# Three attentions written out step by step, with the norm and router of the layer behind each inside its loop

## The chip, the core and the metric

The kernel runs on one core of a Trainium2 chip as one program. The metric is the device time of one execution in microseconds (us). A core has five engines, each with an instruction stream of its own that runs in order: PE (TensorE: matmuls and transposes), DVE (VectorE), ACT (ScalarE), POOL (GpSimd) and SP (SyncE, which here only issues DMAs). They are tied together by semaphores: an instruction that waits holds everything behind it on its engine.

## The reference

Four layers, each `x = x + attention(norm(x))` and then `x = x + ffn(norm(x))`, over 4096 tokens of 128 channels in 64 sequences of 64. The norm has no gain: `(x - mean) / sqrt(var + 1e-5)`. Attentions 1 to 3 are alike but for a mask in the first:

```python
q = split_heads(norm(x) @ Wq + bq)          # 16 heads of 8 channels
attn = softmax(q @ k.T * scale)             # 64 x 64 per head and sequence
x = x + join_heads(attn @ v) @ Wo + bo
```

The ffns behind them (8 experts with 2 per token; 64 grouped experts; 64 experts with a capacity) all begin with a router: `logits = norm(x) @ Wr`, with 8 or 64 columns.

## The kernel before, in words

X stays in SBUF as 32 tiles of 128 tokens. The program is a row of stages: attention 0, its output, ffn 0 (which also writes the keys and values of the three later attentions to DRAM), and then three times: a norm, a plain attention (`attention_rows`; parts at1, at2, at3 of the names in the rows), a norm with router (`layer_norm(..., router=...)`; ln3, ln5, ln7), and an ffn (ex, gr, cap). All engines meet at the end of a stage.

`pipelined` sets the order inside a stage. Each engine has a list of (lead, stage), and in step n runs each stage of the list for tile n + lead. In `attention_rows` of before, the first and last steps are written out and the middle is a loop over four tiles with addresses from a register. The lists of one step n:

- PE: `weigh`(n-1), `turn(0)`(n), `project_out`(n-2), `score`(n+1), `turn(1)`(n), `turn_o`(n-1), `project_q`(n+2).
- ACT: `take_q`(n+1), `take_o`(n-2), `exponent(0)`(n), `exponent(1)`(n).
- DVE: `top`, `shift(0)`, `shift(1)` of n, `weigh_down`(n-1), `measure`(n-3: the norm's sums), `residual`(n-2).
- POOL: `part_heads`(n+1), which multiplies the keys by head masks into KM, and `add_bias`(n+1).
- SP: `load_ahead`(n): keys K(n) after KM(n-4) is made, then values V(n) after `weigh`(n-4). K and V have four slots, and tiles 0 to 3 are loaded with the weights, ahead of the stage.

So `score`(n+1) needs KM(n+1), and that needs K(n+1) landed; K(n+1) is issued some three steps ahead of its use.

The norm with router works on groups of four tiles: DVE makes mean and root for all tiles at once (ACT gives the square root), normalises a group, PE turns it, ACT copies it to xT, PE multiplies by the router's weights, DVE copies the logits. In ln7 SP also writes the normalised rows to DRAM (`cap_rows`), one DMA for four tiles. The weights that the ffn needs (`also=loads`) are issued on SP in this norm's stage.

Of the kernel before, what the change touches and what calls it, by code (L numbers as in the profile page):

```python
# [9 lines left out]

# [536 lines left out]
def attention_rows(nc, m, part, norm, wq, wo, bq, bv, bo, keys, values, keep_mask=None):  # L547
# [8 lines left out]
    with ExitStack() as own:  # L556
# [16 lines left out]
        On, OT = sb("On", [P, HEADS, DH]), sb("OT", [P, P])  # L573
        if keep_mask is not None:
# [7 lines left out]
        def load_keys(sp, i, s):  # L582
            sp.dma_start(K[:, s, :], keys[:, bass.ds(P * i, P)]).then_inc(k_in[s], 16)

        def load_values(sp, i, s):
            v = VZ[:, s, :, :, :].rearrange("p r j w -> p (r j w)")
            sp.dma_start(v, values[bass.ds(i, 1), :, :].rearrange("a p w -> p (a w)")).then_inc(v_in[s], 16)

        def loads(sp):
# [4 lines left out]
            sp.dma_start(bias[:, :], bo.partition_broadcast(P)).then_inc(loaded, 16)  # L594
            if keep_mask is not None:
# [14 lines left out]
        TURNED, Y = slice(0, P), slice(P, 2 * P)  # L610
        chained, prepared, dots_ready = m.sem("chained"), m.sem("prepared"), m.sem("dots_ready")
# [4 lines left out]
        LOADS = 16 * (5 + (2 if keep_mask is not None else 0))  # L616
        run = lambda eng, stages: pipelined(eng, NT, stages, period=SLOTS)

        with nc.Block() as block:
            @block.sync  # L620
            def _(sp):
                def load_ahead(i, s, n):
                    if isinstance(i, int) and i < SLOTS:
# [6 lines left out]
                run(sp, [(0, load_ahead)])  # L630

            @block.gpsimd
            def _(pool):
                pool.wait_ge(prepared, 2)

                def add_bias(i, s, n):
                    mine = m.X[:, bass.ds(i, 1), :].rearrange("p a d -> p (a d)")
# [8 lines left out]
                run(pool, [(1, part_heads), (1, add_bias)])  # L646

            @block.tensor
            def _(pe):
# [3 lines left out]
                def project_q(i, s, n):  # L653
                    wait_past(pe, q_taken, i)
                    pe.matmul(psP[:, 0:P], Wq[:, :], m.xT[:, bass.ds(P * i, P)], start=True, stop=True).then_inc(q_done, 1)
# [47 lines left out]
                run(pe, [(-1, weigh), (0, turn(0)), (-2, project_out), (1, score), (0, turn(1)), (-1, turn_o), (2, project_q)])  # L703

            @block.scalar
            def _(act):
# [20 lines left out]
                run(act, [(1, take_q), (-2, take_o), (0, exponent(0)), (0, exponent(1))])  # L727

            @block.vector
            def _(dve):  # L730
# [1859 lines left out]
```

## Time and profile before

| | us |
|---|---|
| runs (median; lowest, highest) | 2042.02; 2039.81, 2051.98 |
| the profiled execution | 2055.21, of which its span 2053.4 |
| mean granted TensorE clock in it | 0.832 |

The stages around the change in the profiled execution, all times from the span's start:

| | at1 | at2 | at3 |
|---|---|---|---|
| last `top` of the attention starts | 677.73 | 1104.00 | 1708.30 |
| first work of the ffn behind the norm | 713.61 | 1137.43 | 1742.76 |

Between these two times lie the last tile's way through the attention, the meeting of the engines and the norm with router. Times are in us unless marked ns; a granted clock of 1.00 is TensorE at 2.4 GHz, 0.50 at 1.2 GHz, and a value between them is a stretch that held both.

### The profile page before, as it was taken

The numbers are of one execution on the slowest core, as the hardware profiler recorded it, in microseconds if no ns is written. First come the engines' busy times: TensorE is split into PE (matmuls) and PEld (weight loads), VectorE is DVE, ScalarE is ACT, GpSimd is POOL, SyncE is SP. The second block draws the span as 40 slices with busy tenths as digits, with TensorE's granted clock in tenths as the row PEclk, the third lists the DMA queues.
The fourth block names the chain that finished last, engine by engine and source line by source line (L and its number), as shares of the span: only waits on it lengthen the run. The fifth ranks groups of instructions, "written<-read, shape, count | busy, mean of one in ns | idle before, by whom it ended". The sixth has DMA issues, their size and how long they took to land. (4 is left out here: it accounts for less than half of the span.)

```text
span 2053.4 us, 45919 instructions
## 1 busy us (share of the span) xinstructions
PE 1617.8 (79%) x14578; PEld 1144.2 (56%) x14579; DVE 1418.5 (69%) x3509; ACT 825.6 (40%) x1722; POOL 820.6 (40%) x809
## 2 busy tenths in 40 slices
PE   5999953823688888996888699989997987179992
PEld 4777752312566655664666344437996766055551
DVE  6888866957688553437787799986776886943332
ACT  3554532778333222323343577752112343122221
POOL 3888823367233071016331000005774331047883
PEclk8999966955799699998898899999998997555555
DMA  5333302930111151112112477637993111334446
GB/s 139 82 78 78 90 2 63 283 91 0 45 47 46 43 168 39 41 35 57 45 55 58 138 306 307 266 164 263 418 415 123 56 54 52 87 80 81 82 83 149
DMA packets 242442, 241.51 MB, mean 118 GB/s; under 512 B 105698, under 2 KB 225315, under 8 KB 234915
## 3 DMA queue, kind: packets, MB, share of 16 engines
q1 hardware_dynamic: 221074, 221.02, 32.9%
q0 software_dynamic: 14336, 14.69, 3.9%
q10 hardware_dynamic: 6928, 4.49, 0.8%
q8 instruction: 56, 0.92, 0.2%
q14 instruction: 48, 0.39, 0.1%
HBM read 137.28 MB, written 100.24 MB: 116 GB/s over the span
## 5 line engine op out<-in xcount | busy, mean ns | idle before, releaser
L643 POOL TENSOR_TENSOR at_KM<-at_K,at_mask 128x512 f32<-128x512 f32 x96 | 99.8, 1039 | 301.1 <-PE at_psS L668 239.6
L718 ACT ACTIVATE at_ET<-at_psT 128x512 f32<-128x512 f32 x192 | 114.6, 597 | 245.6 <-PE at_psT L677 245.6
L753 DVE TENSOR_REDUCE at_mx<-at_psS 128x16 f32<-128x1024 f32 x96 | 117.6, 1225 | 55.0 <-PE at_psS L668 54.7
L400 POOL TENSOR_TENSOR at_E<-at_Z,at_mx 128x512 f32<-128x512 f32 x128 | 130.7, 1042 | 45.4 <-PE at_psT L445 28.4
L2058 POOL TENSOR_TENSOR gr_work<-gr_ring 128x512 f32<-128x512 f32 x96 | 121.5, 1288 | 51.7 <-DVE gr_work L2092 44.5
L690 PE MATMUL at_psO<-at_VZ,at_ET 128*64 128x18 f32 x3072 | 110.1, 215 | 40.6 <-ACT at_ET L718 40.6
L677 PE MATMUL at_psT<-kept_ident,at_Z 128*128 128x128 f32 x768 | 131.0, 295 | 10.7 <-DVE at_Z L766 5.3
L2142 PEld LDWEIGHTS gr_psY<-gr_wd,gr_work 128*128 128x128 f32 x1024 | 133.8, 192 | 5.9
L2142 PE MATMUL gr_psY<-gr_wd,gr_work 128*128 128x128 f32 x1024 | 135.8, 276 | 0.0
L690 PEld LDWEIGHTS at_psO<-at_VZ,at_ET 128*64 128x64 f32 x3072 | 101.3, 141 | 58.8 <-ACT at_ET L718 37.4
L1936 PE MATMUL gr_psV<-kept_xT,gr_wu 128*128 (+1 forms) x240 | 125.2, 604 | 0.8 <-ACT gr_V L1806 0.8
L1936 PE MATMUL gr_psV<-kept_xT,gr_wg 128*128 (+1 forms) x240 | 124.6, 601 | 0.0
L677 PEld LDWEIGHTS at_psT<-kept_ident,at_Z 128*128 128x128 f32 x768 | 84.0, 145 | 55.0 <-issue 40.2
L518 DVE TENSOR_TENSOR at_Z<-at_psS,at_amask 128x512 f32<-128x512 f32 x128 | 82.5, 686 | 42.6 <-PE at_psS L437 41.5
L2384 POOL DMA_INDIRECT cap_acc<-cap_Y,cap_idx x64 | 101.9, 1592 | 20.7 <-issue 18.9
L2423 DVE TENSOR_TENSOR cap_h<-cap_psU,cap_sg 64x128 f32<-64x128 f32 x64 | 18.1, 282 | 119.7 <-ACT cap_sg L2437 119.7
L2378 POOL DMA_INDIRECT cap_GX<-cap_rows,cap_idx x64 | 63.3, 989 | 90.9 <-DVE cap_idx L2417 77.7
L2059 POOL MEMSET gr_one<- 64x1 f32 x1 | 0.1, 91 | 247.5 <-POOLq L1781 247.5
L1817 ACT ACTIVATE gr_ring<-gr_psV,gr_bu 128x512 f32<-128x512 f32 x120 | 82.4, 687 | 31.3 <-PE gr_psV L1936 31.3
L1817 ACT ACTIVATE gr_ring<-gr_psV,gr_bg 128x512 f32<-128x512 f32 x120 | 82.4, 687 | 23.6 <-PE gr_psV L1936 23.2
L2092 DVE TENSOR_TENSOR gr_work<-gr_psF,gr_work 128x512 f32<-128x512 f32 x96 | 66.0, 688 | 33.1 <-PE gr_psY L2142 22.9
L768 DVE TENSOR_TENSOR at_Z<-at_psS,at_mx 128x512 f32<-128x512 f32 x128 | 82.5, 686 | 6.6
(556 smaller groups left out, 4205.3 us busy)
## 6 DMA issues: line engine op xcount, KB each, us to landing
gr_spill<-gr_ring SPq DMA_DIRECT2D x28, 2048.0 KB, 6.2
gr_ring<-gr_spill SPq DMA_DIRECT2D x28, 2048.0 KB, 10.2
at_amask<-mask_Bx16xSxS_ff SPq DMA_DIRECT2D x128, 128.0 KB, 2.9
kv_values<-bit_VS SPq DMA_DIRECT2D x32, 432.0 KB, 6.5
at_VZ<-kv_values SPq DMA_DIRECT2D x96, 144.0 KB, 2.1
kv_keys<-bit_KS SPq DMA_DIRECT2D x8, 768.0 KB, 6.9
at_K<-kv_keys SPq DMA_DIRECT2D x96, 64.0 KB, 1.9
cap_acc<-cap_zero SPq DMA_DIRECT2D x2, 2112.0 KB, 12.6
```

The costliest lines, as they stand in the source:

```text
L400: pool.tensor_tensor(E[:, a, :].rearrange("p (v k) -> p v k", k=SEQ), Z[:, s % 2, a, :].rearrange("p (v k) -> p v k", k=SEQ), mx[:, s % 2, ...
L518: dve.tensor_tensor(Z[:, s % 2, a, :].rearrange("p (g h e k) -> p g h e k", g=2, h=2, e=2), psS[:, 2 * a:2 * a + 2, 0:256].rearrange("p g ...
L643: pool.tensor_tensor(KM[:, s % 2, :, :], K[:, s, :].unsqueeze(1).broadcast_to([P, 4, P]), mask4[:, :].unsqueeze(2).broadcast_to([P, 4, P]) ...
L677: last = pe.transpose(psT[:, r * P:r * P + P], Z[:, a, r * P:r * P + P], m.ident[:, :])
L690: last = pe.matmul(psO[rows, t * PW:t * PW + PW], ET[:, 4 * a + r, rows], VZ[:, s, PAIRS * b + t, :, :].rearrange("p j w -> p (j w)"), sta ...
L718: act.activation(ET[:, 4 * a:4 * a + 4, :].rearrange("p r q -> p (r q)"), psT[:, :], ACT.Exp, scale=QK_SCALE).then_inc(exped, 1)
L753: dve.tensor_reduce(mx[:, :].rearrange("p (g v) -> p g v", v=4), psS[:, :, 0:256].rearrange("p g (v k) -> p g v k", k=SEQ), AX.X, ALU.max) ...
L1817: act.activation(ring[:, u, j % TILES, :], psV[:, j % 4, :], ACT.Silu if is_up else ACT.Identity, bias=bias).then_inc(taken, 1)
L1936: pe.matmul(psV[:, j % 4, :], w, m.xT[:, bass.ds(512 * g, 512)], start=True, stop=True).then_inc(multiplied, 1)
L2058: pool.tensor_tensor(tp[:, s % 4, :], ring[:, s // 4, first, :], ring[:, s // 4, first + 1, :], ALU.mult).then_inc(pooled, 1)
L2142: last = pe.matmul(psY[:, j, :], h[:, s % 2, j * P:j * P + P], wd[:, s, :], start=False, stop=(s == C - 1), skip_group_check=True)
L2384: pool.indirect_dma_start(accs[s % ACCS], bass.IndirectOffsetOnAxis(ap=idx2[:, s:s + 1], axis=0), Y[:, s % 4, :], None, compute_op=ALU.add ...
```

## The change

`attention_rows` is written out for all tiles, without a loop. The three norms with router are gone as stages; their work stands in the attention's lists, tile by tile: `aggregate` on DVE (-3), a reciprocal root by Newton steps on POOL for each group of four tiles (`invert`, -4; the last group by DVE behind its list), `normalise` on ACT (-9), `turn_hat` on PE (-10), `take_hat` on ACT (-10), `route` on PE (-10), `take_logits` on ACT (-11). On SP the ffn's loads stand ahead of `load_ahead`, and in at3 `write_row`(-9) stands behind it. The calls and some buffers move accordingly.

```diff
+def invert_std(eng, chain, m, g, moments, shift, work):
+    mine = slice(4 * g, 4 * g + 4)
+    v, y, t = (work[:, n, :] for n in range(3))
+    chain.link(eng.tensor_scalar(v, moments[:, mine, 1], EPS, None, ALU.add))
+    eng.tensor_scalar(y.bitcast(I32), v.bitcast(I32), -0.5, GUESS, ALU.mult, ALU.add)
+    chain.link(eng.tensor_scalar(v, v, -0.5, None, ALU.mult))
+    for _ in range(3):
+        chain.link(eng.tensor_tensor(t, y, y, ALU.mult))
+        chain.link(eng.tensor_tensor(t, t, v, ALU.mult))
+        chain.link(eng.tensor_scalar(t, t, 1.5, None, ALU.add))
+        chain.link(eng.tensor_tensor(y, y, t, ALU.mult))
+    eng.tensor_scalar(m.rstd[:, mine], y, 1.0, None, ALU.mult)
+    eng.tensor_scalar(m.mean[:, mine], moments[:, mine, 0], 1.0, None, ALU.mult)
+    chain.link(eng.tensor_tensor(t, moments[:, mine, 0], y, ALU.mult))
+    return eng.tensor_scalar(shift[:, mine], t, -1.0, None, ALU.mult)
...
+        xh, newton = sb("xh", [P, SLOTS, D]), sb("newton", [P, 2, 3, 4])
...
-        run = lambda eng, stages: pipelined(eng, NT, stages, period=SLOTS)
+        run = lambda eng, stages: pipelined(eng, NT, stages, period=SLOTS, unrolled=True)
...
                 def load_ahead(i, s, n):
-                    if isinstance(i, int) and i < SLOTS:
+                    if i < SLOTS:
                         return
                     sp.wait_ge(km_ready, i - (SLOTS - 1))
                     load_keys(sp, i, s)
                     sp.wait_ge(summed, i - (SLOTS - 1))
                     load_values(sp, i, s)
 
-                run(sp, [(0, load_ahead)])
+                def write_row(i, s, n):
+                    if rows is not None:
+                        sp.wait_ge(hat_ready, i + 1)
+                        sp.dma_start(rows[i], xh[:, s, :]).then_inc(rows_out[s], 16)
+
+                if also:
+                    also(sp)
+                run(sp, [(0, load_ahead), (-9, write_row)])
...
-                run(pool, [(1, part_heads), (1, add_bias)])
+                def invert(i, s, n):
+                    if s == SLOTS - 1 and n < LAST:
+                        pool.wait_ge(moments_ready, i + 1)
+                        invert_std(pool, newtons, m, n, moments, shift_by, newton[:, 0]).then_inc(inverted_std, 1)
+
+                run(pool, [(1, part_heads), (1, add_bias), (-4, invert)])
...
-                run(pe, [(-1, weigh), (0, turn(0)), (-2, project_out), (1, score), (0, turn(1)), (-1, turn_o), (2, project_q)])
+                def turn_hat(i, s, n):
+                    pe.wait_ge(hat_ready, i + 1)
+                    wait_past(pe, logits_taken, i)
+                    pe.transpose(psP[:, HAT], xh[:, s, :], m.ident[:, :]).then_inc(hat_turned, 1)
+
+                def route(i, s, n):
+                    pe.wait_ge(hat_taken, i + 1)
+                    pe.matmul(psP[:, LOGITS], m.xT[:, P * i:P * i + P], Wr[:, :], start=True, stop=True).then_inc(routed, 1)
+
+                run(pe, [(-1, weigh), (0, turn(0)), (-2, project_out), (1, score), (-10, turn_hat), (0, turn(1)), (-1, turn_o),
+                         (-10, route), (2, project_q)])
...
-                run(act, [(1, take_q), (-2, take_o), (0, exponent(0)), (0, exponent(1))])
+                def normalise(i, s, n):
+                    if n < LAST:
+                        act.wait_ge(inverted_std, n + 1)
+                    else:
+                        act.wait_ge(inverted_last, 1)
+                    wait_past(act, hat_turned, i - (SLOTS - 1))
+                    if rows is not None:
+                        wait_past(act, rows_out[s], 16 * n)
+                    act.activation(xh[:, s, :], m.X[:, i, :], ACT.Identity, bias=shift_by[:, i:i + 1], scale=m.rstd[:, i:i + 1]).then_inc(hat_ready, 1)
...
+                run(act, [(1, take_q), (-11, take_logits), (-2, take_o), (-9, normalise), (0, exponent(0)), (-10, take_hat), (0, exponent(1))])
...
-                run(dve, [(0, top), (0, shift(0)), (0, shift(1)), (-1, weigh_down), (-3, measure), (-2, residual)])
+                run(dve, [(0, top), (0, shift(0)), (0, shift(1)), (-1, weigh_down), (-3, measure), (-2, residual), (-3, aggregate)])
+                dve.wait_ge(moments_ready, NT)
+                invert_std(dve, chain, m, LAST, moments, shift_by, newton[:, 1]).then_inc(inverted_last, 1)
...
-        layer_norm(nc, m, "ln3", router=(t["L1_ffn_w_router"], prob), also=loads)
+        attend(router=(t["L1_ffn_w_router"], prob), also=loads)
...
-            layer_norm(nc, m, "ln5", router=(t["L2_ffn_Wr"], S), also=loads)
+            attend(router=(t["L2_ffn_Wr"], S), also=loads)
...
-            layer_norm(nc, m, "ln7", router=(t["gate_wT"], L), rows=tiles_of(rows)[:, :, 0:D])
+            attend(router=(t["gate_wT"], L), rows=tiles_of(rows)[:, :, 0:D])
```

Three places show how instructions move. The first is SP in at3, the end of its list before: keys (L583) and values (L587) alone, then the stage ends, and the norm's stage loads its router weights (L200) and writes the rows (L206).

```order
L583 DMA at_K<-kv_keys 128x128
L587 ISA
L587 DMA at_VZ<-kv_values 128x288
L121 REGISTER_ALU
L121 COMPARE_AND_BRANCH
L619 UNCONDITIONAL_BRANCH
L197 UNCONDITIONAL_BRANCH
L200 DMA ln7Wr<-gate_wT 128x64
L206 DMA cap_rows<-ln7xh 128x4x128 x8
```

SP in at3 after the change: keys (L610), values (L614) and row writes (L667), from K(8) to the third row.

```order
L610 DMA at_K<-kv_keys 128x128
L614 DMA at_VZ<-kv_values 128x288
L610 DMA at_K<-kv_keys 128x128
L614 DMA at_VZ<-kv_values 128x288
L667 DMA cap_rows<-at_xh 128x128
L610 DMA at_K<-kv_keys 128x128
L614 DMA at_VZ<-kv_values 128x288
L667 DMA cap_rows<-at_xh 128x128
L610 DMA at_K<-kv_keys 128x128
L614 DMA at_VZ<-kv_values 128x288
L667 DMA cap_rows<-at_xh 128x128
```

Six pairs of K and V (tiles 4 to 9) come without a row. From K(10) on one row write stands ahead of every K: row n-9, then K(n+1), V(n+1), row n-8. Twenty-two of K(10) to K(31) stand so, and the last ten rows follow together.

The second is ACT in at3, one step. Before: the take of q (L712), of the turned output (L725), and the two halves of the exponential (L718).

```order
L712 ACTIVATE at_Q<-at_psP,at_bq 128x128
L725 ACTIVATE at_OT<-at_psY 128x128
L718 ACTIVATE at_ET<-at_psT 128x512 x2
L712 ACTIVATE at_Q<-at_psP,at_bq 128x128
L725 ACTIVATE at_OT<-at_psY 128x128
L718 ACTIVATE at_ET<-at_psT 128x512 x2
```

And after, where `cap_L` is the logits, `at_xh` the normalised tile and `kept_xT` its turned copy:

```order
L772 ACTIVATE at_Q<-at_psP,at_bq 128x128
L803 ACTIVATE cap_L<-at_psP 128x64
L785 ACTIVATE at_OT<-at_psY 128x128
L795 ACTIVATE at_xh<-kept_X,at_shift,kept_rstd 128x128
L778 ACTIVATE at_ET<-at_psT 128x512
L799 ACTIVATE kept_xT<-at_psP 128x128
L778 ACTIVATE at_ET<-at_psT 128x512
```

The normalised tile is the fourth instruction behind the second exponential of the step before, and the first exponential of its own step comes behind it.

The third is PE in at3, one step after the change; without L756 (`turn_hat`) and L760 (`route`) it is the step of before.

```order
L740 MATMUL at_psO<-at_VZ,at_ET 64x18 x16
L727 MATMUL at_psT<-kept_ident,at_Z 128x128 x4
L751 MATMUL at_psY<-at_Wo,at_OT 128x128
L718 MATMUL at_psS<-at_KM,at_Q 64x256 x8
L756 MATMUL at_psP<-kept_ident,at_xh 128x128
L727 MATMUL at_psT<-kept_ident,at_Z 128x128 x4
L747 MATMUL at_psY<-kept_ident,at_On 128x128
L760 MATMUL at_psP<-at_Wr,kept_xT 128x64
L705 MATMUL at_psP<-kept_xT,at_Wq 128x128
```

`turn_hat` came between the score of tile n+1 and the second turn of tile n, `route` ahead of the projection of q.

## Rows read from the trace of the kernel before

**Rows 1.** Windows: us, busy (x count) of PE, PEld, DVE, ACT, POOL, PEclk, DMA, GB/s.

```profile
420.00:510.00 90.00, 30.00 (x232) 22.37 (x232) 60.06 (x146) 74.14 (x93) 75.06 (x32) 0.50 0.08 21
677.70:713.60 35.90, 28.05 (x181) 25.62 (x180) 16.75 (x63) 8.69 (x16) 0.00 (x0) 0.55 0.09 25
1104.00:1137.40 33.40, 20.61 (x181) 18.44 (x179) 18.15 (x62) 8.70 (x16) 0.00 (x0) 0.77 0.59 105
1603.00:1708.00 105.00, 93.45 (x1655) 74.13 (x1647) 91.80 (x189) 43.70 (x108) 37.74 (x52) 1.00 0.19 53
1708.30:1742.80 34.50, 26.14 (x181) 24.08 (x179) 18.23 (x62) 8.73 (x17) 0.04 (x1) 0.61 0.21 63
```

**Rows 2.** Timeline of at3, DVE: `top` of tiles 4 and 31 (start, duration).

```profile
1603.25 1.23 DVE L753 TENSOR_REDUCE at_mx<-at_psS 128x16 f32<-128x1024 f32 x1 [0.39 <-PE at_psS L668]
...
1708.30 1.23 DVE L753 TENSOR_REDUCE at_mx<-at_psS 128x16 f32<-128x1024 f32 x1 [0.29 <-PE at_psS L668]
```

**Rows 3.** Timeline of one step of at3 at full clock.

```profile
1651.20 1.11 PE L690 MATMUL at_psO<-at_VZ,at_ET 128*64 128x18 f32 x32 [0.55 <-ACT at_ET L718]
...
1652.49 0.33 SPq L587 DMA_DIRECT2D at_VZ<-kv_values  x1
...
1653.05 0.69 PE L668 MATMUL at_psS<-at_KM,at_Q 32*64 32x256 f32 x16
...
1653.36 0.34 SPq L583 DMA_DIRECT2D at_K<-kv_keys  x1
...
1653.67 0.65 PE L677 MATMUL at_psT<-kept_ident,at_Z 128*128 128x128 f32 x4
...
1653.95 1.04 POOL L643 TENSOR_TENSOR at_KM<-at_K,at_mask 128x512 f32<-128x512 f32 x1 [2.56 <-PE at_psS L668]
...
1654.36 0.60 ACT L718 ACTIVATE at_ET<-at_psT 128x512 f32<-128x512 f32 x1 [0.83 <-PE at_psT L677]
1654.85 0.36 ACT L712 ACTIVATE at_Q<-at_psP,at_bq 128x128 f32<-128x128 f32 x1
...
1655.10 0.28 ACT L725 ACTIVATE at_OT<-at_psY 128x128 f32<-128x128 f32 x1
```

**Rows 4.** Timeline of one step of at2 at half clock.

```profile
987.34 1.16 PE L668 MATMUL at_psS<-at_KM,at_Q 32*64 32x256 f32 x16
...
988.42 1.11 PE L677 MATMUL at_psT<-kept_ident,at_Z 128*128 128x128 f32 x4
...
989.54 0.64 PE L655 MATMUL at_psP<-kept_xT,at_Wq 128*128 128x128 f32 x2
...
990.21 0.37 ACT L712 ACTIVATE at_Q<-at_psP,at_bq 128x128 f32<-128x128 f32 x1
```

**Rows 5.** ACT's normalise in ln6, durations in ns min/median/max.

```profile
L265 ACT ACTIVATE ln6xh<-kept_X,ln6shift,kept_rstd x8: 479/492/505, 1572.3 to 1578.2; 128x128 f32<-128x128 f32 x8
```

**Rows 6.** Timeline of ln7, PE: eight router passes, two for a tile.

```profile
1724.54 1.80 PE L300 MATMUL ln7psL<-ln7Wr,kept_xT 128*128 128x64 f32 x8
```

**Rows 7.** DMA issues, all K loads: count, KB, median us to landing.

```profile
at_K<-kv_keys SPq DMA_DIRECT2D x96, 64.0 KB, 1.9
```

**Rows 8.** The first four K loads of at2, each with a V load behind it.

```profile
L583 SPq DMA_DIRECT2D at_K<-kv_keys x4: 431/432/442, 966.8 to 969.7; - x4
...
DMA to landing us min/median/max: 2.8/3.2/3.5
```

**Rows 9.** Timeline of at1's end: the last tile's output turned, and added to X.

```profile
686.44 0.18 PEld L697 LDWEIGHTS at_psY<-kept_ident,at_On 128*128 128x128 f32 x1 [0.74 <-DVE at_On L776]
...
688.11 0.29 DVE L782 TENSOR_TENSOR kept_X<-kept_X,at_psY 128x128 f32<-128x128 f32 x1 [1.46 <-PE at_psY L701]
```

**Rows 10.** Timeline of ln5, SP: first and last of the grouped ffn's loads.

```profile
1114.54 0.43 SPq L1753 DMA_DIRECT2D gr_br<-L_ffn_br  x1
...
1136.25 0.53 SPq L1762 DMA_DIRECT2D gr_bd<-L_ffn_bdown  x1
```

**Rows 11.** Costliest groups: POOL's smallest operation, us and mean ns.

```profile
L1611 POOL TENSOR_TENSOR ex_spare<-ex_zero 128x1 f32<-128x1 f32 x32 | 6.5, 203 | 138.4 <-DVE ex_idx L1636 137.8
```

More of the change, by code:

```diff
@@ L9 @@
 from contextlib import ExitStack
+from functools import partial
 import concourse.bass as bass
@@ L544, in _, with attention_rows @@
                 run(dve, [(0, add_masks), (-2, invert), (0, top(0)), (-2, weigh_down), (0, top(1)), (-2, add_halves)])
-def attention_rows(nc, m, part, norm, wq, wo, bq, bv, bo, keys, values, keep_mask=None):
+GUESS = float(0x5F3759DF)
+def invert_std(eng, chain, m, g, moments, shift, work):
[13 more added lines that the diff above has]
+    return eng.tensor_scalar(shift[:, mine], t, -1.0, None, ALU.mult)
+def attention_rows(nc, m, part, norm, wq, wo, bq, bv, bo, keys, values, keep_mask=None, *, router, also=None, rows=None):
     m.part = part
@@ L573, in attention_rows @@
         On, OT = sb("On", [P, HEADS, DH]), sb("OT", [P, P])
+        wr, logits = router
+        E = logits.shape[2]
+        Wr = sb("Wr", [P, E])
+        xh, newton = sb("xh", [P, SLOTS, D]), sb("newton", [P, 2, 3, 4])
+        moments, shift_by = sb("moments", [P, NT, 2]), sb("shift", [P, NT])
         if keep_mask is not None:
@@ L615, in attention_rows @@
         y_ready, x_added = m.sem("y_ready"), m.sem("x_added")
-        LOADS = 16 * (5 + (2 if keep_mask is not None else 0))
-        run = lambda eng, stages: pipelined(eng, NT, stages, period=SLOTS)
+        measured, moments_ready, newton_chained, inverted_std, inverted_last, hat_ready = (m.sem(n) for n in (
+            "measured", "moments_ready", "newton_chained", "inverted_std", "inverted_last", "hat_ready"))
+        hat_turned, hat_taken, routed, logits_taken = (m.sem(n) for n in ("hat_turned", "hat_taken", "routed", "logits_taken"))
+        rows_out = [m.sem(f"rows_out{u}") for u in range(SLOTS)] if rows is not None else None
+        LAST = NT // 4 - 1
+        LOADS = 16 * (6 + (2 if keep_mask is not None else 0))
+        run = lambda eng, stages: pipelined(eng, NT, stages, period=SLOTS, unrolled=True)
         with nc.Block() as block:
@@ L628, in load_ahead @@
                     load_values(sp, i, s)
-                run(sp, [(0, load_ahead)])
+                def write_row(i, s, n):
[5 more added lines that the diff above has]
+                run(sp, [(0, load_ahead), (-9, write_row)])
+                for s in range(SLOTS if rows is not None else 0):
+                    sp.wait_ge(rows_out[s], 16 * NT // SLOTS)
             @block.gpsimd
@@ L1745, in grouped_ffn @@
             eq, sel, rank, excl = (sb(n, [P, NG], on=routing) for n in ("eq", "sel", "rank", "excl"))
-            ones = sb("ones", [P, HALF], on=routing)
             count, cols = sb("count", [P, 4], on=routing), sb("cols", [P, 8], on=routing)
@@ L2525, in program @@
         m.free_sems()
-        attention_rows(nc, m, "at1", "ln2", *(t["L1_xattn_" + n] for n in ("wq", "wo", "bq", "bv", "bo")), keys[0], values[:, 0],
-                  keep_mask=t["mask_1x1xSxS2_ik1"])
+        attend = partial(attention_rows, nc, m, "at1", "ln2", *(t["L1_xattn_" + n] for n in ("wq", "wo", "bq", "bv", "bo")),
+                         keys[0], values[:, 0], keep_mask=t["mask_1x1xSxS2_ik1"])
+        expert_ffn(nc, m, t, attend)
         m.free_sems()
-        expert_ffn(nc, m, t)
+        attend = partial(attention_rows, nc, m, "at2", "ln4", *(t["L2_xattn_" + n] for n in ("WqT", "WoT", "Wq_b", "Wv_b", "Wo_b")),
+                         keys[1], values[:, 1])
+        grouped_ffn(nc, m, t, attend)
         m.free_sems()
-        attention_rows(nc, m, "at2", "ln4", *(t["L2_xattn_" + n] for n in ("WqT", "WoT", "Wq_b", "Wv_b", "Wo_b")), keys[1], values[:, 1])
-        m.free_sems()
-        grouped_ffn(nc, m, t)
-        m.free_sems()
-        attention_rows(nc, m, "at3", "ln6", *(t["L3_xattn_" + n] for n in ("Wq", "Wo", "bq", "bv", "bo")), keys[2], values[:, 2])
-        m.free_sems()
-        capacity_ffn(nc, m, t)
+        attend = partial(attention_rows, nc, m, "at3", "ln6", *(t["L3_xattn_" + n] for n in ("Wq", "Wo", "bq", "bv", "bo")),
+                         keys[2], values[:, 2])
+        capacity_ffn(nc, m, t, attend)
 def lay_out(inputs):
```

33 lines of the change are left out of this document (23 added, 10 removed).

## The prediction, as recorded before the changed kernel was run

> **What bounds the kernel now.** I read three views: the windows by stage, then the timeline of single steps, then the DMA and group lists. The windows [rows 1] give two kinds of stretch. In the loop of at3 PE is busy 93.45 of 105 us at clock 1.00, DVE 91.80; the two engines hand each other one tile after the other, and a tile takes (1708.30 - 1603.25) / 27 = 3.89 us [rows 2]. Behind the last tile come 35.9, 33.4 and 34.5 us of drain, engines' meeting and router norm, in which PE works 20.6 to 28.1 us, much of it at half clock. These 103.8 us are what the change can shorten; the loops are what it can lengthen, 96 tiles in all. One step of at3 [rows 3] shows what is not on the path now: K's issue at 1653.36 is for a tile three steps ahead, and KM at 1653.95, which starts when a buffer comes free (2.56 us behind PE), is for the score after next. So the chain from K over KM to the score has more than two steps in hand.
>
> The trace has another thing that matters: SP is one stream. V's issue at 1652.49 comes 0.18 us after `weigh` ends (1651.20 + 1.11), for it waits for a `weigh`, and the next K, whose own wait was over long before, is issued only behind it at 1653.36 [rows 3]. A wait of SP holds what is queued behind it.
>
> **The drains.** Removed: three norms with router as stages. Added: the last tiles' norm in the drain of the attention. The last `top` of at1 starts at 677.73, and the last residual ends at 688.40 [rows 9], 10.7 us later. Behind it the lists go on to lead -11, nine steps more. Each is PE turn, ACT copy, PE route, ACT copy, one after the other, since `turn_hat` waits for the logits of the tile before. The nearest rows are turn, copy, projection, add: 686.44 to 688.11, 1.67 us, and 0.30 for the last operation, so 1.97 at half clock. With 0.9 for the aggregate and the end (estimate: three operations of the size of the DVE row) [rows 9] the drain is 10.7 + 9 x 1.97 + 0.9 = 29.3 us. The same is taken for all three: saved are 6.6, 4.1 and 5.2, together **15.9 us**. Bounds: nothing saved; or the PE half of each round (0.9 us) halved at full clock, some 4 us more each. DVE's own inversion of the last group lies beside the first of these rounds, which still handle earlier tiles; without that cover it would add about 4 us a drain.
>
> **The loops of at1 and at2.** PE gets one transpose (a quarter of 0.65 = 0.16 us) ahead of `turn(1)`, and the router pass in a gap in which PE waits for ACT anyway. ACT gets three operations, and is idle over half of the time [rows 1]. What goes is the loop's own register work; I put the step at 3.94 against 3.89 us, 27 x 0.05 = **+1.4** in at2, and nothing in at1, whose mask makes its step longer. DVE's aggregate lies in the wait of DVE for the score (0.29 to 0.39 us) [rows 2]. If it didn't fit, it would cost about 0.2 x 96 = 19 us, which I hold unlikely.
>
> POOL's inversion is 19 small operations for four tiles. The smallest POOL operation in the trace takes 203 ns [rows 11]: 3.9 us at least; with a hand-over of 0.1 us (taken) at each of 15 chained ones 5.4; with the 0.21 that POOL took to follow PE (1653.74 to 1653.95) [rows 3] 7.0. It starts behind the aggregate, some 0.75 us after a score's start, and KM (1.04, and 0.2 to start) must be made two scores later: 2 x 3.89 - 0.75 - 1.24 = 5.8 us. So at 5.4 it is hidden and costs nothing; the cover is thin.
>
> **The ffn's loads.** In at2 SP now issues the grouped ffn's weights ahead of K(4): 1114.54 to 1136.78 in the trace, 22.2 us [rows 10]. Until K(4) is needed there are four tiles preloaded, four steps of 3.9 to about 6 us at half clock, and the pipeline's start. K(4) comes late by 0 to 6.6 us; **+3**.
>
> **The row writes in at3.** Before, eight DMAs behind the loop; now 32. For 22 tiles, K(10) to K(31), the write of row n-9 stands on SP ahead of K(n+1). It waits for `normalise`(n-9), which ACT does in step n, as the fourth instruction behind the last exponential of step n-1. K(n+1) must then be issued, land, be made into KM and scored, all in that same step n, since PE's list has `score`(n+1) ahead of `turn(1)`(n). The three steps in hand are gone, and a closed ring is left, one turn for a tile: score, `turn_hat`, `turn(1)`, exponential, `take_q`, `take_logits`, `take_o`, `normalise`, row issue, K issue, landing, KM, score. Behind SP's wait stands K, and for K wait POOL, PE and so all.
>
> At full clock [rows 3]: score to `turn(1)` 0.62, `turn_hat` 0.16, `turn(1)` to the end of the exponential 1.29 (1653.67 to 1654.96). `take_q` starts 0.11 before that end, the three behind it at 0.25 each (1654.85 to 1655.10), and `normalise` takes 0.49 [rows 5]: 1.13. SP: 0.18 to wake, 0.48 from one issue to the next (966.8 to 969.7 holds six) [rows 8], landing 2.2. The landing has a median of 1.9 when K goes nearly alone [rows 7] and 2.8 to 3.5 in a burst of eight [rows 8]; here K has one row write ahead of it and one V behind, nearer to alone. So 2.86. KM 1.04 and two hand-overs, 0.15 together (PE to ACT took 0.04, PE to POOL 0.21): 1.19. Sum 0.62 + 0.16 + 1.29 + 1.13 + 2.86 + 1.19 = **7.25 us**, 3.36 more than 3.89.
>
> At half clock [rows 4]: 1.08 and a quarter of 1.11 to `turn(1)`. Then `project_q` ends last: 989.54 + 0.64 - 988.42 = 1.76, with a router pass ahead of it (1.80 / 4 = 0.45) [rows 6]; `take_q` 0.03 later, 0.75 and 0.49 to the end of `normalise`. With SP and POOL as above: 1.08 + 0.28 + 1.76 + 0.45 + 0.03 + 0.75 + 0.49 + 2.86 + 1.19 = **8.89 us**, 5.00 more.
>
> Which clock? In the ring PE stands still for the 4 us from `normalise` to KM in every step. The stretches of the trace with such gaps ran at 0.50, 0.55, 0.61 and 0.77, the dense loop at 1.00 [rows 1]. I take half clock: 22 x 5.00 = **+110**.
>
> The Trainium skill has a sentence that speaks against a cost here: in "Trainium Kernel Development and Optimization", Key Constraints, it says that DMAs issued from several engines run on the same 16 DMA engines, and that spreading them saves only the sequencer's issue time. By that, rows on SP cost SP's issue time alone, and the +110 would be nothing. V ahead of K [rows 3] shows that the wait in front of an issue also counts.
>
> **Sum.** -15.9 + 1.4 + 3 + 110 = +98.5, and a few tenths for the ten other steps of at3: +99. The profiled execution is 2055.2 us (span 2053.4 and 1.8 around it), which makes 2154; it lies 13 us above the median of the runs, 2042.0, for which I get **2141 us**. Its own range: landing 1.9 to 3.2 gives -7 to +22, the drains -13 to +16, K(4) 3 either way; not all at one end, 2129 to 2165.
>
> **The rivals.**
> 1. The ring turns at full clock: 22 x 3.36 = 74 in place of 110, **2105 us** (2093 to 2129). For it: PE's work in a step is dense once it starts. Against it: the windows named above. Chance 0.20.
> 2. POOL is late too. If a chained operation costs the 0.21 hand-over, the inversion takes 7.0 us against 5.8 of cover, and 1.2 us are lost for each of seven groups in at1 and at2 (at3 has time to spare): +17, **2158 us**. It decides at 5.8 us. For it: no chain of small POOL operations is in the trace. Against it: the 203 ns. Chance 0.12.
> 3. Not slower: SP's wait for the row is over before K is due, so that the rows cost 22 x 0.48 = 11 us of an SP that is idle anyway. The place is K's issue in at3. What decides is the time from `normalise` to the score, 2.86 + 1.19 = 4.05 us. Between the end of the exponential (1654.96) and the score one step after 1653.05 lie about 2.0 us, and `normalise` itself ends 1.13 after the exponential, so 0.9 us are there for 4.05. For it: the sentence above, and that K was three steps early. Then -15.9 + 4.4 + 1.4 = -10 is left: **2032 us**. Chance 0.08.
> 4. The norm inside the drain saves nothing, the ring is there: +16 on the forecast, inside its range; no chance of its own.
>
> **How the numbers follow.** Half clock 0.60, full clock 0.20, POOL late 0.12, rows harmless 0.08. The range 2093 to 2168 takes in the first two with their bounds and most of the third, and leaves out the last. A measurement of this kernel can tell about 1% (20 us) from no change: 2032 is within it, and faster only if the drains come out at their best too. Faster 0.03, within 1% 0.06, slower 0.91.
>
> **What would show it.** In at3 of the changed kernel the distance between two `top`s should be 3.9 us up to about tile 9 and then 8.9 (7.25 at clock 1.00) to tile 31, each K issue right behind a row issue, each row issue waiting for `normalise`, POOL's KM waiting for K's landing and no more for PE, and the granted clock down to 0.50. At2 should keep 3.9 to 4.0 and begin with one gap at tile 4. From last `top` to the ffn's first work there should be about 29 us. The forecast is wrong if the `top`s of at3 stay at 4 us, if KM still waits for PE there, or if POOL's inversion shows up as a wait for KM in every fourth step of at2.

## The result, and the profile after

| | us |
|---|---|
| kernel before: median (lowest, highest) | 2044.98 (2039.81, 2051.98) |
| changed kernel: median (lowest, highest) | 2128.59 (2126.46, 2133.61) |
| ratio, 95% interval | 1.041 [1.037, 1.045] |
| forecast (range) | 2141 (2093 to 2168) |
| profiled execution of the changed kernel, span, clock | 2126.46, 2124.7, 0.808 |

The change makes the kernel 4.1% slower. Where the time goes is read from a few marks in both traces: the first and the last `top` of each attention, and the first work of the ffn behind it.

| us | before | after | difference |
|---|---|---|---|
| start to the norm ahead of at1 (nothing changed there) | 520.8 | 514.5 | -6.3 |
| at1, first to last `top` | 141.85 | 139.42 | -2.4 |
| at2, first to last `top` | 125.48 | 136.81 | +11.3 |
| at3, first to last `top` | 123.21 | 217.45 | +94.2 |
| last `top` to the ffn, at1, at2, at3 | 35.9, 33.4, 34.5 | 25.1, 25.7, 29.5 | -10.8, -7.7, -4.9 |
| all else (norms ahead, the three ffns) | | | -2.1 |
| span | 2053.4 | 2124.7 | +71.3 |

The windows of the changed kernel (start:end, us, busy of PE, PEld, DVE, ACT and POOL, granted clock, DMA share, GB/s) show at2's loop, at3's ring and the three drains.

```profile
1003.00:1096.90 93.90, 91.58 (x1526) 72.98 (x1525) 84.73 (x193) 57.25 (x158) 56.13 (x158) 1.00 0.19 52
1606.00:1786.00 180.00, 137.28 (x1402) 109.22 (x1401) 79.72 (x177) 54.12 (x150) 52.25 (x142) 0.57 0.13 35
1786.00:1815.50 29.50, 21.30 (x121) 15.70 (x121) 8.59 (x37) 11.99 (x40) 3.28 (x16) 0.50 0.08 23
1096.90:1122.60 25.70, 16.33 (x121) 11.34 (x119) 8.44 (x37) 11.78 (x40) 3.71 (x19) 0.67 0.00 1
668.80:693.90 25.10, 16.09 (x121) 11.90 (x121) 8.72 (x38) 11.27 (x40) 3.65 (x19) 0.64 0.00 1
```

At2's loop is as dense as at3's was [rows 1], with the norm's work in it. At3 is another stretch: PE idle for 43 of 180 us and its clock down to 0.57, while DMA has less to do than before (35 against 53 GB/s). No engine is busy throughout and no DMA is the bound there; something waits. One turn at half clock, from the timeline, chosen rows in order of time:

```profile
1740.27 0.50 ACT L795 ACTIVATE at_xh<-kept_X,at_shift,kept_rstd 128x128 f32<-128x128 f32 x1
1740.79 0.32 SPq L667 DMA_DIRECT2D cap_rows<-at_xh  x1
1741.15 0.43 SPq L610 DMA_DIRECT2D at_K<-kv_keys  x1
...
1743.17 1.04 POOL L686 TENSOR_TENSOR at_KM<-at_K,at_mask 128x512 f32<-128x512 f32 x1 [6.60 <-DMA at_K<-kv_keys]
...
1744.27 1.16 PE L718 MATMUL at_psS<-at_KM,at_Q 32*64 32x256 f32 x16 [1.26 <-POOL at_KM L686]
...
1745.36 0.47 PE L756 MATMUL at_psP<-kept_ident,at_xh 128*128 128x128 f32 x1
...
1745.62 1.06 PE L727 MATMUL at_psT<-kept_ident,at_Z 128*128 128x128 f32 x4
...
1747.01 0.68 PE L705 MATMUL at_psP<-kept_xT,at_Wq 128*128 128x128 f32 x2
...
1747.73 0.37 ACT L772 ACTIVATE at_Q<-at_psP,at_bq 128x128 f32<-128x128 f32 x1 [0.41 <-PE at_psP L705]
...
1748.26 0.50 ACT L795 ACTIVATE at_xh<-kept_X,at_shift,kept_rstd 128x128 f32<-128x128 f32 x1
...
1748.78 0.32 SPq L667 DMA_DIRECT2D cap_rows<-at_xh  x1
```

Read the starts from top to bottom: each row follows the one above it, when that has ended or landed; PE's rows overlap a little, and short ones that are not shown lie between some of them. `normalise` ends at 1740.77, the row is issued 0.02 us later, K 0.36 after it, KM starts 2.02 us after K's issue, the score 1.10 after KM's start, and 8.0 us after the first row write comes the next. Against the step of before [rows 3], KM no longer waits for PE to free a buffer but for K's landing. The same holds for all tiles of the ring. The view of POOL's KM gives how often it ran, what ended POOL's idle time before it, and who waited for it (total us, times):

```profile
L686 POOL TENSOR_TENSOR at_KM<-at_K,at_mask x22: 1040/1040/1041, 1610.0 to 1783.6; 128x512 f32<-128x512 f32 x22
...
  DMA at_K<-kv_keys: 121.9, 22
...
  PE at_psS L718: 42.3, 22
```

All 22 KMs wait for K, 121.9 us together, and 22 scores wait for KM, 42.3 us. K itself is not slow to land:

```profile
L610 SPq DMA_DIRECT2D at_K<-kv_keys x22: 320/432/865, 1608.1 to 1781.7; - x22
...
DMA to landing us min/median/max: 1.8/2.0/3.4
```

A median of 2.0 us against 1.9 before [rows 7]: it is issued late. The distance between `top`s is 3.8 us from the fourth to the ninth step, then 6.6, and from there between 7.9 and 9.5; 8.19 on average over the 22 steps between these two:

```profile
1605.78 1.23 DVE L831 TENSOR_REDUCE at_mx<-at_psS 128x16 f32<-128x1024 f32 x1 [0.30 <-PE at_psS L718]
...
1786.00 1.23 DVE L831 TENSOR_REDUCE at_mx<-at_psS 128x16 f32<-128x1024 f32 x1 [2.04 <-PE at_psS L718]
```

In the longest steps K landed later. In the one of 9.24 us it took 3.2 us from K's issue to KM:

```profile
1632.54 0.43 SPq L610 DMA_DIRECT2D at_K<-kv_keys  x1
...
1635.73 1.04 POOL L686 TENSOR_TENSOR at_KM<-at_K,at_mask 128x512 f32<-128x512 f32 x1 [2.46 <-DMA at_K<-kv_keys]
```

At2 lost 11 us at one place, its fifth tile. SP and POOL there:

```profile
959.40 7.99 SPq L1840 DMA_DIRECT2D gr_wg<-L_ffn_Wgate  x1
967.85 6.83 SPq L1841 DMA_DIRECT2D gr_wd<-L_ffn_Wdown  x1
...
976.84 0.52 SPq L1844 DMA_DIRECT2D gr_bd<-L_ffn_bdown  x1
977.41 0.58 SPq L610 DMA_DIRECT2D at_K<-kv_keys  x1
...
981.83 1.04 POOL L686 TENSOR_TENSOR at_KM<-at_K,at_mask 128x512 f32<-128x512 f32 x1 [15.90 <-DMA at_K<-kv_keys]
...
984.19 1.22 DVE L831 TENSOR_REDUCE at_mx<-at_psS 128x16 f32<-128x1024 f32 x1 [8.23 <-PE at_psS L718]
```

K(4) is issued behind the grouped ffn's weights and lands 4.4 us later, beside their traffic (DMA is busy 0.82 of this step). The step is 11.75 us long, and three more follow at 6.2 us, at half clock:

```profile
984.20:1002.80 18.60, 18.46 (x184) 14.51 (x184) 10.95 (x25) 5.19 (x12) 5.39 (x11) 0.50 0.13 35
```

The kernel before has 125.48 in the table, and some 4 us of it are a start of at2 at half clock (steps of 5.76 and 6.19), which this execution of the changed kernel did not have; the run with the loads behind, below, is the cleaner comparison.

### The profile page after: what moved, and what is told of

Its sections match the earlier page's. It is cut to its first block and busy times, and to the rows that moved or that the text cites. A ratio compares the mean times of both kernels' runs of the same rounds, so it can differ in the third digit from the quotient of the medians.

```text
span 2124.7 us, 45141 instructions
## 1 busy us (share of the span) xinstructions
PE 1668.8 (79%) x14578; PEld 1171.9 (55%) x14579; DVE 1400.7 (66%) x3518; ACT 887.1 (42%) x1978; POOL 902.0 (42%) x1208
## 5 line engine op out<-in xcount | busy, mean ns | idle before, releaser
L727 PE MATMUL at_psT<-kept_ident,at_Z 128*128 128x128 f32 x768 | 147.0, 323 | 7.3 <-DVE at_Z L844 2.9
L740 PE MATMUL at_psO<-at_VZ,at_ET 128*64 128x18 f32 x3072 | 123.7, 226 | 12.7 <-ACT at_ET L778 10.6
L740 PEld LDWEIGHTS at_psO<-at_VZ,at_ET 128*64 128x64 f32 x3072 | 113.9, 157 | 31.9 <-ACT at_ET L778 27.6
L718 PE MATMUL at_psS<-at_KM,at_Q 32*64 32x256 f32 x1536 | 81.5, 487 | 51.0 <-POOL at_KM L686 51.0
L727 PEld LDWEIGHTS at_psT<-kept_ident,at_Z 128*128 128x128 f32 x768 | 101.8, 164 | 28.3 <-issue 16.9
L2507 DVE TENSOR_TENSOR cap_h<-cap_psU,cap_sg 64x128 f32<-64x128 f32 x64 | 18.1, 283 | 118.4 <-ACT cap_sg L2521 118.4
```

Source lines behind the costliest of these rows:

```text
L727: last = pe.transpose(psT[:, r * P:r * P + P], Z[:, a, r * P:r * P + P], m.ident[:, :])
L740: last = pe.matmul(psO[rows, t * PW:t * PW + PW], ET[:, 4 * a + r, rows], VZ[:, s, PAIRS * b + t, :, :].rearrange("p j w -> p (j w)"), sta ...
```

## The experiments

The theory: at3's loss is the wait of SP for the normalised row, with K queued behind it, and at2's is K(4) behind the weights. The rivals: the row writes cost by issue and traffic; the written-out code or the added work on ACT and PE is slow in itself; the half clock is a cause of its own. Ratios are to the kernel before, run beside each; the `top` distances are of one profiled execution each.

**Keys ahead.** SP's loads three tiles earlier; row writes, their place and their waits untouched.

```diff
-                run(sp, [(0, load_ahead), (-9, write_row)])
+                run(sp, [(3, load_ahead), (-9, write_row)])
```

> The changed kernel, with one number changed: SP's list runs the K and V loads three tiles ahead (lead 3 in place of 0). The row write of at3 keeps its place on SP, its wait for the normalised tile and its traffic. Theory (a row's wait on SP holds K back, and a ring score - normalise - row - K - KM - score is left): K(n+3) is now issued behind row n-10 and has two steps in hand, so at3's 22 steps fall from 8.19 us to 3.9: 22 x 4.3 = 94 us less, about 2034 us. Rival (the 32 row writes cost by their own issue and traffic, or ACT's and PE's added work makes the step long): nothing of that has changed, the steps stay near 8.2 and the time near 2128.

Measured: 2032.41 us, ratio 0.991 [0.989, 0.994]. At3's steps are 3.81 and 3.92, its `top`s 123.36 us apart in place of 217.45. POOL's waits in 70 us of at3 (total us, times, longest):

```profile
POOL at_newton L555 <- DVE at_moments L868: 10.6, 5, 2.1
POOL at_KM L686 <- PE at_psS L718: 9.9, 4, 2.5
```

KM waits for PE again, as before the change [rows 3], and never for K between the first and the last `top` of at3, though one K took 3.9 us to land. SP still waits for every row; nobody needs what stands behind it at once. All 94 us of at3 are gone with one number.

**Rows later.** Eight buffers for normalised tiles, the row written three steps later, between the same K loads.

```diff
-        xh, newton = sb("xh", [P, SLOTS, D]), sb("newton", [P, 2, 3, 4])
+        HATS = 2 * SLOTS
+        xh, newton = sb("xh", [P, HATS, D]), sb("newton", [P, 2, 3, 4])
...
-                run(sp, [(0, load_ahead), (-9, write_row)])
+                run(sp, [(0, load_ahead), (-12, write_row)])
```

> The changed kernel with the normalised tiles in eight buffers in place of four, and the row write of at3 at lead -12 in place of -9: the same 32 DMAs at the same place between the K loads on the same queue, but each for a tile that was normalised three steps before. Theory (it is the wait for normalise that holds SP): the wait is over when SP comes to it, K is on time, at3's steps fall to 3.9 us, about 2034 us. Rival (issue and traffic of the rows): 8.2 us a step and 2128 stay. If both the wait and the issue count, the steps come out between, by 0.4 to 0.5 us for each row issue: 2044.

Measured: 2030.95 us, 0.993 [0.990, 0.996]; steps 3.81 and 3.92. SP's timeline in the ring:

```profile
1651.14 0.32 SPq L615 DMA_DIRECT2D at_VZ<-kv_values  x1
1651.50 0.43 SPq L668 DMA_DIRECT2D cap_rows<-at_xh  x1
...
1651.97 0.43 SPq L611 DMA_DIRECT2D at_K<-kv_keys  x1
```

The row stands ahead of K as in the changed kernel and costs 0.47 us of SP, and no step is longer for it. So it is the wait, and not the row's issue or traffic.

**Rows from ACT.** The same writes on ACT's queue, behind the second exponential.

```diff
-                run(sp, [(0, load_ahead), (-9, write_row)])
+                run(sp, [(0, load_ahead)])
...
+                def write_row(i, s, n):
+                    if rows is not None:
+                        act.wait_ge(hat_ready, i + 1)
+                        act.dma_start(rows[i], xh[:, s, :]).then_inc(rows_out[s], 16)
...
-                run(act, [(1, take_q), (-11, take_logits), (-2, take_o), (-9, normalise), (0, exponent(0)), (-10, take_hat), (0, exponent(1))])
+                run(act, [(1, take_q), (-11, take_logits), (-2, take_o), (-9, normalise), (0, exponent(0)), (-10, take_hat), (0, exponent(1)), (-9, write_row)])
```

> The changed kernel with the 32 row writes of at3 issued by ACT, behind the second exponential of the step that normalised the tile, in place of SP; K and V alone on SP. Theory (K is held back by the wait that stands ahead of it in the same stream): the ring opens, at3's steps fall to 3.9 to 4.3 us (ACT spends 0.3 to 0.4 us on each issue and was idle 0.6 us or more before each exponential), 2030 to 2042 us. Rival, after the sentence of the Trainium skill that another issuing engine saves only the sequencer's issue time: 22 x 0.36 = 8 us less, about 2120 us.

Measured: 2031.06 us, 0.992 [0.989, 0.995]; at3's steps 3.92. Another queue gave 97 us, not the 8 of the issue time. The sentence of the Trainium skill ("Trainium Kernel Development and Optimization", Key Constraints) that issuing from several engines saves only the sequencer's issue time gives no more than those 8; here the measurement decides against it as a price. In "DMA: Bandwidth & Descriptors" (Anatomy of one DMA — SWDGE (gpsimd) path) the Trainium skill says that a semaphore wait happens on the issuing sequencer, before dispatch. That section is on DMAs of GpSimd; the trace shows the same for SP, where the row's issue follows the end of `normalise` by 0.02 us (1740.77, 1740.79) and K's comes 0.36 behind it.

**Clock fill.** The changed kernel with five idle matmuls a step on PE ahead of the score, in at3 from tile 10 on.

```diff
+                def fill(i, s, n):
+                    if rows is not None and i >= 10:
+                        for _ in range(5):
+                            pe.matmul(psP[:, 3 * P:4 * P], m.ident[:, :], m.ident[:, :], start=True, stop=True)
...
-                run(pe, [(-1, weigh), (0, turn(0)), (-2, project_out), (1, score), (-10, turn_hat), (0, turn(1)), (-1, turn_o),
+                run(pe, [(-1, weigh), (0, turn(0)), (-2, project_out), (0, fill), (1, score), (-10, turn_hat), (0, turn(1)), (-1, turn_o),
```

> The changed kernel, and in at3 from tile 10 on five more matmuls a step on PE ahead of the score, whose result nobody uses: they fill the gap in which PE waits for KM. The ring stays as it is. Theory (part of the ring's 8.19 us is TensorE's half clock, which the gaps bring about): the granted clock of at3's ring rises from 0.57 to near 1.00 and the step falls to about 6.7 us (the forecast's 7.25 for full clock less the 0.5 us by which the trace's SP part is shorter), 22 x 1.5 = 33 us less: about 2096 us. Rival (the clock is not what the gaps decide, or the ring's length is all in SP, ACT and POOL): the clock stays near 0.57, the added matmuls lie in the gap or lengthen the step by up to 2 us: 2128 to 2170.

Measured: 2110.61 us, 1.031 [1.027, 1.035], so 18 us less than the changed kernel (ratio 1.041), with more work. The window of the ring, and one turn in it:

```profile
1612.00:1772.00 160.00, 121.33 (x1609) 101.12 (x1609) 77.84 (x176) 54.07 (x150) 51.60 (x140) 0.90 0.14 40
1701.66:1708.28 6.62, 5.07 (x78) 4.21 (x75) 3.54 (x9) 2.50 (x7) 1.45 (x2) 1.00 0.14 42
```

The granted clock went from 0.57 to 0.90, and the step from 8.19 to 7.30 us ((1772.1 - 1611.5) / 22). The turn shown lies between two row writes, 6.62 us apart, wholly at clock 1.00. So the theory's 6.7 is there, in some of the steps. The others are longer for two reasons: three steps of about 8 us ran at clock 0.54 to 0.57, and in five steps of 7.4 to 8.1 us at clock 1.00 K took 2.9 to 3.5 us to land in place of 2.0. Of the 4.3 us that a step of the ring lost, 1.4 are the half clock (8.0 against 6.62, K landing in 2.0 us in both), some 0.2 what later landings add on average (8.19 against 8.0), and 2.7 the ring itself, which is there at either clock.

**Loads behind.** The changed kernel with the ffn's weights behind the K and V loads.

```diff
-                if also:
-                    also(sp)
                 run(sp, [(0, load_ahead), (-9, write_row)])
+                if also:
+                    also(sp)
```

> The changed kernel with the ffn's weight loads of SP behind the K and V loads in place of ahead of them; at3's rows as in the changed kernel. Theory (the grouped ffn's weights hold K(4) of at2 back by 7 us and the half clock then lasts three tiles longer): at2 goes back from 136.8 us between its first and last top to about 126, so 10 us less, 2118 us. Rival (the weights are needed at the ffn's start and only wait in another place): the grouped ffn begins late by what at2 gains, and the time stays at 2128.

Measured: 2119.67 us, 1.035 [1.030, 1.040]. At2's `top`s are 121.35 us apart in place of 136.81; the fifth step is 3.81 us long in place of 11.75, and no half clock follows. So K(4) behind the weights is the cause of at2's loss. The stretch gains 15.5 us where 10 were expected; the medians differ by 9, as do the two profiled executions, in which the unchanged part ahead of at1 took 3.3 us more here and the grouped ffn 2.5. That ffn took 433.3 to 436.1 us whether the loads stood ahead or behind (436.1 in keys ahead, too), so that it waits for its weights is not what shows; the gain stays.

**Unrolled only.** The kernel before with its attentions written out, and nothing else (the same edit as in the change: `unrolled=True` and constant addresses).

```diff
-        run = lambda eng, stages: pipelined(eng, NT, stages, period=SLOTS)
+        run = lambda eng, stages: pipelined(eng, NT, stages, period=SLOTS, unrolled=True)
```

> The kernel before, with its three attentions written out without a loop and with constant addresses, and nothing else: the norms with router stay stages of their own. Theory (the loop's registers cost little and its removal gains little: the changed kernel's at1 lost 2.4 us between first and last top): steps of 3.81 in place of 3.89 us in 24 steps of each of three attentions, 5 to 6 us less, 2039 us. Rival (written-out code is slow in itself, for there are more instructions to fetch, and that is part of the loss): more than 2045 us.

Measured: 2036.75 us, 0.997 [0.994, 1.000]: no slower, and not surely faster. The steps of at2 and at3 are 3.81 and 3.82, as expected, where the loop had 4.00 at every second pair. Written-out code is no part of the loss. Beside the 3.92 of the changed kernel it also prices the norm inside the loop: 0.11 us a step in at2, and nothing in at1 (4.51 here, 4.41 to 4.51 in the changed kernel).

**Long inverse.** Keys ahead, and six Newton steps in place of three, to measure the cover over POOL's inversion.

```diff
-    for _ in range(3):
+    for _ in range(6):
         chain.link(eng.tensor_tensor(t, y, y, ALU.mult))
```

> The kernel with K and V three tiles ahead on SP, and six Newton steps in place of three in the inversion (twelve more chained operations of 0.28 us: POOL's inversion takes 8.6 us in place of 5.2; the last group's, on DVE, about 2.4 us more). It measures the cover over POOL's inversion. By the forecast's 5.8 us of cover POOL would make KM 2.8 us late once in four steps, 7 x 2.8 us in each of at1, at2 and at3: 59 us more than 2032, about 2090 us. Rival (KM is made a tile further ahead than the forecast took, so the cover is 9 us or more): 2032 to 2036 us, with no wait for KM on PE.

Measured: 2136.85 us, 1.043 [1.038, 1.048]: 104 us slower than keys ahead, more than either expected. In at2 every fourth step is 6.4 us long and the one behind it mostly 5.7 to 6.7. PE's waits in 100 us of at2 (total us, times, longest), then the clock in a window of at2 and in two steps, one with such a wait and the one behind it:

```profile
PE at_psS L718 <- POOL at_KM L686: 9.1, 4, 2.6
```

```profile
1060.00:1130.00 70.00, 63.11 (x826) 51.01 (x825) 45.99 (x104) 32.00 (x90) 37.73 (x120) 0.77 0.15 42
...
1052.78:1059.15 6.37, 3.95 (x66) 3.10 (x66) 3.55 (x9) 2.50 (x7) 5.21 (x20) 1.00 0.19 56
1059.15:1065.39 6.24, 6.24 (x65) 4.93 (x65) 3.64 (x8) 2.50 (x7) 2.38 (x4) 0.54 0.10 27
```

From the inversion's first operation to the KM behind it POOL takes 8.6 us here, and in at2 and at3 PE then mostly waits 2.4 for that KM (1.7 to 2.6). So the cover in at2 is about 8.6 - 2.4 = 6.2 us, near the forecast's 5.8, and the rival's 9 was wrong. The waits of all three attentions are 17, together 36 us (six in at1, six in at2, five in at3; the seventh inversion of an attention has no KM behind it), while the `top`s of the three lie 96 us further apart than in keys ahead. The rest came with the clock, in the step of the wait or the one to three behind it, which ran wholly or partly at half clock: a gap of PE in a dense loop cost 2.7 times its length here.

**Both moved.** Keys ahead and loads behind.

```diff
-                if also:
-                    also(sp)
-                run(sp, [(0, load_ahead), (-9, write_row)])
+                run(sp, [(3, load_ahead), (-9, write_row)])
+                if also:
+                    also(sp)
```

> The changed kernel with the K and V loads three tiles ahead on SP and the ffn's weight loads behind them, nothing else. Theory (the two losses stand in different places and add): 2032 less the 10 us of at2: about 2022 us, 1.2% under the kernel before, with steps of 3.8 to 3.9 us in at2 and at3 and no gap at at2's fifth tile. Rival (what at2 gains is given back because the weights come late for the grouped ffn): 2032 us.

Measured: 2021.88 us, 0.988 [0.985, 0.991]. At2 121.36 us, at3 123.27: the two losses add. The change is worth 1.2% once SP's list is in order, against 0.3% for the written-out loops alone.

**Drain overlapped.** Both moved, and the last ten tiles turn and route in the banks of the scores, the router pass one step later.

```diff
+        FREE = NT - 10
+        hat_at = lambda i: psP[:, P:2 * P] if i < FREE else psS[:, i % 4, 0:P]
+        logits_at = lambda i: psP[:, 2 * P:2 * P + E] if i < FREE else psS[:, i % 4, P:P + E]
+        early = lambda stage: lambda i, s, n: stage(i, s, n) if i < FREE else None
+        late = lambda stage: lambda i, s, n: stage(i, s, n) if i >= FREE else None
...
-                         (-10, route), (2, project_q)])
+                         (-10, early(route)), (-11, late(route)), (2, project_q)])
...
-                run(act, [(1, take_q), (-11, take_logits), (-2, take_o), (-9, normalise), (0, exponent(0)), (-10, take_hat), (0, exponent(1))])
+                run(act, [(1, take_q), (-11, early(take_logits)), (-12, late(take_logits)), (-2, take_o), (-9, normalise), (0, exponent(0)), (-10, take_hat), (0, exponent(1))])
```

> As the kernel with both loads moved, and the last ten tiles of each attention turn and route in the four PSUM banks that the scores have left free, with the router pass one step behind the turn, so that PE turns tile i+1 while ACT copies tile i. Theory (the drain is a chain PE - ACT - PE - ACT of 1.8 to 1.9 us a tile, nine times in each attention): a round falls to about 1.2 us, 9 x 0.6 x 3 = 16 us less, one round more of 1.2 x 3 = 4 us: 12 us less, about 2010 us. Rival (PE alone takes 1.1 us a round at half clock and ACT 1.0, and the rounds in the first half lie beside the last tile's attention, so little is left): 2022 us.

Measured: 2000.41 us, 0.977 [0.973, 0.980], the fastest of all, and 21.5 us less than both moved, where 12 were expected. One round of the drain in the changed kernel (at3), and then in this one:

```profile
1802.90 0.69 PE L760 MATMUL at_psP<-at_Wr,kept_xT 128*128 128x64 f32 x2 [0.37 <-ACT kept_xT L799]
1803.62 0.22 ACT L803 ACTIVATE cap_L<-at_psP 128x64 f32<-128x64 f32 x1 [0.78 <-PE at_psP L760]
1803.74 0.48 ACT L795 ACTIVATE at_xh<-kept_X,at_shift,kept_rstd 128x128 f32<-128x128 f32 x1
...
1803.99 0.45 PE L756 MATMUL at_psP<-kept_ident,at_xh 128*128 128x128 f32 x1 [0.41 <-ACT cap_L L803]
...
1804.48 0.28 ACT L799 ACTIVATE kept_xT<-at_psP 128x128 f32<-128x128 f32 x1 [0.25 <-PE at_psP L756]
```

```profile
1688.11 0.60 PE L764 MATMUL at_psS<-at_Wr,kept_xT 128*128 128x64 f32 x2
1688.19 0.48 ACT L799 ACTIVATE at_xh<-kept_X,at_shift,kept_rstd 128x128 f32<-128x128 f32 x1
1688.58 0.27 ACT L803 ACTIVATE kept_xT<-at_psS 128x128 f32<-128x128 f32 x1
...
1688.73 0.47 PE L760 MATMUL at_psS<-kept_ident,at_xh 128*128 128x128 f32 x1
1688.75 0.22 ACT L807 ACTIVATE cap_L<-at_psS 128x64 f32<-128x64 f32 x1
...
1689.00 0.59 PE L764 MATMUL at_psS<-at_Wr,kept_xT 128*128 128x64 f32 x2
```

In the first, leaving out the normalise (L795), each row waits for the one above it, and a round takes 1.91 us. In the second, ACT works beside PE, and this round takes 0.89 at the same half clock; those of at3 take 0.67 to 0.88 from logits to logits. Once in each drain 1.8 to 2.3 us pass: the normalise of the last group now waits for DVE's inversion (1.2 us in at3), which the slower rounds had covered. From last `top` to ffn there are 17.8, 17.9 and 18.1 us in place of 24.8, 25.3 and 25.3 in both moved: 21.6 us, as much as the medians differ. The two profiled executions differ by 14.2 us only, for at1 and at2 of this one began with steps at half clock and are 11.7 us longer from first to last `top`.

## Why the prediction was right, and where its sizes were off

**The ring in at3: right, 15 us too large.** Forecast 22 x 5.00 = 110 at half clock, measured 22 x 4.30 = 95 (8.19 - 3.89). Its start at tile 10, its members and KM's wait came as described, and the three kernels that part K from the row's wait take it away. The size: from `normalise`'s end to KM's start the sum had 2.86; the trace has 2.40 (0.02 to wake, 0.36 to K's issue, 2.02 to land). From `take_q` to `normalise` ACT takes 0.53 (1747.73 to 1748.26), not three times 0.25, when the inputs are ready; KM and its hand-over take 1.10, not 1.19. That is 0.77 of the 0.9 us by which the quiet steps of 8.0 are below 8.89; steps of 8.4 to 9.5, in most of which K took 2.4 to 3.4 us to land, make the 8.19. Such landings are there in keys ahead too (up to 3.9 us) and cost nothing there; the ring puts each of them on the path.

**The clock: right for most of the stretch, for a reason that was too strong.** 0.57 was granted; 15 of the 22 steps ran at 0.50. But PE does not stand still for 4 us a step: `weigh`, the first `turn` and `project_out` lie in that gap, and PE was idle for 43 of 180 us, 1.9 a step. The forecast chose the clock by likeness to the windows of [rows 1], and the choice came out; the length of the standstill it had wrong. The rival at full clock (7.25 us a step, 2105 us) did not come about; filled, a full-clock step is 6.62, with the same 0.6 us too much in the sum.

**The drains: 23.4 saved, 15.9 forecast.** The round was forecast at 1.97 and took 1.77 in at1 and 1.91 in at2 and at3. At3, wholly at half clock, came out at 29.5 against 29.3, and that close only by luck: the last residual ended 12.8 us behind the last `top` in place of 10.7, and eight full rounds of 1.91 followed in place of nine of 1.97. In at1 and at2 the first rounds lie beside the last tile's own way through the attention (there are eight left when it is through, not nine), at a clock of 0.64 and 0.67, so they end 4 us earlier.

**At2's loads: the term that failed.** Forecast +3 with an upper bound of 6.6; the stretch lost 11.3, and 15.5 against the kernel with the loads behind. Two parts were missing: K(4) lands 4.4 us after its issue beside the weights' traffic, not 1.9, and behind the gap of PE that it leaves three more tiles run at half clock. The bound counted the issue time alone.

**The loops and POOL: right but for at1.** Steps of 3.92 in at2 (3.94 forecast); what the loop's registers cost, 0.08, and what the norm adds, 0.11, nearly cancel. At1 was put at nothing and gained 2.4. The inversion, from its first operation to the KM behind it, takes 5.2 us (5.4 forecast):

```profile
1033.87 0.23 POOL L555 TENSOR_SCALAR at_newton<-at_moments 128x4 f32<-128x4 f32 x1 [2.14 <-DVE at_moments L868]
...
1038.88 0.22 POOL L566 TENSOR_SCALAR at_shift<-at_newton 128x4 f32<-128x4 f32 x1
1039.07 1.04 POOL L686 TENSOR_TENSOR at_KM<-at_K,at_mask 128x512 f32<-128x512 f32 x1
```

PE waits for no KM in at2's loop, so it is hidden. By the long inverse the cover is about 6.2 us and not 5.8, so 1.0 us of it is left; and a late POOL would have cost more than the rival's sum, which counts the waits alone (six a stretch, not seven) and no half clock behind them.

**The sum.** The loss was 84 us in the medians (2128.59 - 2044.98); in the profiled pair it is 71.3 + 6.3 = 77.6 us behind the unchanged front. The forecast was 99, put on a median of 2042.02 from three runs; with a fourth the median of the kernel before is 2044.98. From that to 77.6 lead the ring (-16), the drains (-7.5), at1's loop (-2.4), the rest (-2.1) and, the other way, at2 (+6.9: 11.3 in place of 3 + 1.4). The 6.9 us that were missing in at2 hid a part of what the ring and the drains had too much, so the sum came out better than its terms, by luck.

## What to carry to other kernels

When a DMA with a wait is put into a queue, look at what stands behind it and when that is needed: a wait in front of a prefetch can turn it into a load on demand, and whatever makes the wait end then joins a ring with whatever needs the load. Moving the prefetch ahead in the list, or the waiting write back by a few steps, costs a number or a buffer. And price a gap of PE in a dense loop with the steps that follow it: at2's late K cost 1.3 to 2.2 times its gap in four of the kernels here, and the long inverse 2.7 times its gaps.

## What the runs showed of the hardware

- A late arrival costs at the clock as well: behind one 8 us gap at2 ran three steps at clock 0.50, 6.2 us each in place of 3.8; behind gaps of 7.7 to 8.6 us at the same place it was one step in rows later, two in keys ahead and four in rows from ACT.
- Two queued DMAs of SP are issued 0.36 us apart when SP has just waited (1740.79, 1741.15) and 0.47 when it hasn't; SP's issue follows the end of ACT's `normalise` by 0.02 to 0.03 us, and the end of PE's `weigh` by 0.18 [rows 3].
- Large loads hold SP itself, and what is queued behind them: the issues of the grouped ffn's gate and down weights took 7.99 and 6.83 us of its time each, against 0.43 for small ones.
- Small POOL operations of 128 x 4 elements take 0.19 to 0.23 us, and chained by semaphores they start 0.28 to 0.31 apart.
